# A four-deep ring of decays, residual sums in the matrix engine, and a plain fp32 gated layer in a Mamba block

## The reference, cut to what matters

```python
# x: (8, 512, 128) float32; D_INNER = 256, D_STATE = 16, DT_RANK = 64, HIDDEN = 384
h   = x * rsqrt(mean(x * x) + 1e-5) * norm_w
xs, res = split(h @ in_proj_w.T)
u   = silu(causal_depthwise_conv(xs, taps=4) + conv_b)
delta, Bm, Cm = split(u @ x_proj_w.T, [64, 80])
delta = softplus(delta @ dt_proj_w.T + dt_proj_b)
state[t] = exp(delta * A) * state[t-1] + delta * u * Bm      # 256 x 16 states, over 512 steps
y   = (sum_n state * Cm + u * D) * silu(res)
x1  = layernorm(x + (y @ out_proj_w.T + x))
gate, up = x1 @ w_gate.T, x1 @ w_up.T                         # int weights, scaled by 1/127
out = layernorm(x1 + (silu(gate) * up) @ w_down.T)
```

## Time and profile before

| what | us |
|---|---|
| median of three runs (609.94 to 611.24) | 610.42 |
| the profiled execution's own time | 610.23 |
| its span in the trace | 608.5 |
| DVE busy | 534.5 (88% of the span) |
| PE busy | 425.8 (70%) |
| POOL busy | 398.3 (65%) |
| ACT busy | 355.9 (58%) |
| mean granted TensorE clock | 0.838 of full |

### The profile page before, as it was taken

How to read it: one execution, slowest core, us unless ns; L and a number is a source line. 1 busy time by engine, 2 the same in 40 slices (tenths; PEclk the granted TensorE clock), 3 DMA queues, 4 the chain that set the end, 5 groups by cost and what they waited for, 6 DMA issues and landing times.

```text
span 608.5 us, 5732 instructions
## 1 busy us (share of the span) xinstructions
PE 425.8 (70%) x1477; PEld 172.9 (28%) x1477; DVE 534.5 (88%) x582; ACT 355.9 (58%) x594; POOL 398.3 (65%) x176
## 2 busy tenths in 40 slices
PE   4898586786598595887598695887597694467353
PEld 3332121322232241323232241322242241113142
DVE  4779997989998998989998999989998999999822
ACT  2675874496547675496547775497537774443221
POOL 5588597567776777576776688566776688575000
PEclk9988886997988987987988787987988787777756
DMA  8084044300660044400560043400660044400000
GB/s 213 2 180 98 0 89 95 93 1 1 137 152 5 1 99 80 114 0 0 138 151 4 0 97 93 103 0 0 138 155 0 0 99 92 103 1 0 17 1 18
DMA packets 27360, 39.11 MB, mean 64 GB/s; under 512 B 3816, under 2 KB 10056, under 8 KB 27344
## 3 DMA queue, kind: packets, MB, share of 16 engines
q1 hardware_dynamic: 25424, 38.51, 28.0%
q10 hardware_dynamic: 1920, 0.42, 0.4%
HBM read 3.27 MB, written 2.10 MB: 9 GB/s over the span
## 4 chain that ended last, share of the span: by engine, by line
DVE 37%; issue 22%; POOL 16%; PE 10%; ACT 7%; SPq 4%; DMA 3%; DVEq 1%; POOLq 0%; ACTq 0%
DVE state L904 19%; POOL prod L742 11%; DVE weighted L913 9%; SPq L326 4%; DMA du_rep<-z_wm 2%; PE dense_ps L449 2%; DVE g L920 1%; POOL rs L762 1%; ACT decay_ps L554 1%; DVE g_act L955 1%; PE dense_ps L447 1%; PE y_ps L427 1%; ACT L578 1%; ACT x L565 1%; DVE g_act L951 1%
## 5 line engine op out<-in xcount | busy, mean ns | idle before, releaser
L904 DVE TENSOR_TENSOR_SCAN state<-decay_ps,prod 128x512 f32<-128x512 f32 x256 | 299.2, 1208 | 32.1 <-ACT decay_ps L554 16.7
L742 POOL TENSOR_TENSOR prod<-du_rep,b_rep 128x2048 f32<-128x2048 f32 x63 | 284.8, 4530 | 41.5 <-DVE state L904 35.7
L554 ACT ACTIVATE decay_ps<-delta_rep,a_neg 128x512 f32<-128x512 f32 x252 | 169.8, 687 | 74.6 <-DVE state L904 74.2
L913 DVE TENSOR_TENSOR weighted<-state,c_ps 128x2048 f32<-128x2048 f32 x64 | 146.4, 2287 | 2.7 <-DVE state L904 0.6
L416 PE MATMUL c_ps<-xd,pick 96*128 96x512 f32 x128 | 84.4, 747 | 86.3 <-DVE weighted L913 86.3
L427 PE MATMUL y_ps<-weighted,gather 128*32 128x512 f32 x512 | 87.2, 760 | 6.4 <-DVE weighted L913 6.4
L762 POOL TENSOR_TENSOR rs<-ve,powm 128x4 f32<-128x4 f32 x16 | 16.2, 1012 | 104.5 <-ACT nm L560 104.5
L447 PE MATMUL dense_ps<-h_t,tap_t 128*128 128x512 f32 x128 | 58.9, 604 | 6.5 <-ACT h_t L599 6.5
L416 PEld LDWEIGHTS c_ps<-xd,pick 96*128 96x128 f32 x128 | 25.0, 222 | 120.0 <-DVE weighted L913 111.9
L559 ACT ACTIVATE ve<-mv 128x4 f32<-128x4 f32 x16 | 3.3, 206 | 71.4 <-DVE mv L939 44.1
L746 POOL TENSOR_TENSOR z_wm<-z_e,z_wm 128x512 f32<-128x512 f32 x15 | 18.7, 1269 | 30.3 <-ACT z_wm L622 25.3
(11 more groups left out here) (125 smaller groups left out, 550.0 us busy)
## 6 DMA issues: line engine op xcount, KB each, us to landing
du_rep<-z_wm SPq DMA_DIRECT2D x64, 256.0 KB, 5.0
delta_rep<-z_ln SPq DMA_DIRECT2D x64, 256.0 KB, 4.8
out_dram<-y_out SPq DMA_DIRECT2D x8, 256.0 KB, 4.6
state<-L_attn_in_proj_w_in ACTq DMA_DIRECT2D x1, 256.0 KB, 4.1
x_all<-L_attn_x_in SPq DMA_DIRECT2D x1, 256.0 KB, 4.5
weighted<-L_ffn_w_gate_in SPq DMA_DIRECT2D x1, 192.0 KB, 10.7
weighted<-L_ffn_w_up_in SPq DMA_DIRECT2D x1, 192.0 KB, 4.3
weighted<-L_ffn_w_down_in SPq DMA_DIRECT2D x1, 192.0 KB, 5.1
```

The source lines that it names most:

```text
L554: A(decay_ps[n % DECAYS][:, :], decay_ps[n % DECAYS][:, :] if spread_first else delta_rep[:, h, c, :], ACT.Exp, scale=a_neg[:, col:col + 1 ...
L742: TT(prod[quad % 2][:, :, :], du_rep[:, h, :, :], b, ALU.mult).then_inc(prod_ready, 1)
L904: dve.tensor_tensor_scan(state[:, n % BLOCKS, :], decay_ps[n % DECAYS][:, :], prod[n // BLOCKS % 2][:, n % BLOCKS, :], 0.0, ALU.mult, ALU. ...
L913: TT(weighted[quad % 2][:, :, :], state[:, :, :], c_ps[:, :].unsqueeze(1).broadcast_to([P, BLOCKS, T]), ALU.mult).then_inc(weighted_ready, 1)
```

## The change

Seven edits. (1) The ring has four places; the fourth, for groups with n % 4 = 3 (the last of each quad, since 32 is a multiple of 4), is `decay_sb` in SBUF. (2) 2x is added by PE, a matmul of a matrix `twice` (2 on the diagonal) with x into the projection's bank; ACT copies the sum to `r1` at step 6, DVE takes statistics at step 7 (after group 7) and aggregates at 8, ACT's `shift_scale` is at step 9. (3) `down` is one job in one bank with x1 added by a matmul with the identity, and `down_t` is scaled when it is made; statistics and the last normalisation read PSUM, and r2 is gone. (4) Gate and up take x1 whole in fp32, so `x1_hi`, `x1_lo` and L943 are gone. (5) In the first pass POOL does `soften` and `scale_u` of half 1 of sample 0 after the multiply of quad 2 and not before the first products. (6) ACT's `late_copies` follow group 1 and not 0, and decay 3 is spread into the first bank ahead of C. (7) POOL's `scale_shift` of the first norm comes after multiply 3 and not 2. The state buffer stays single.

```diff
 EPS = 1e-5
-DECAYS = 3
+DECAYS = 4
...
     out_t = sb("out_t", [P, HALVES, M])
-    gate_t = sb("gate_t", [M, HID, P], f32r)
-    up_t = sb("up_t", [M, HID, P], f32r)
+    gate_t = sb("gate_t", [M, HID, P])
+    up_t = sb("up_t", [M, HID, P])
...
-    decay_ps = [pb(f"decay_ps{i}") for i in range(DECAYS)]
+    decay_ps = [pb(f"decay_ps{i}") for i in range(DECAYS - 1)]
+    decay = decay_ps + [sb("decay_sb", [P, T])]
...
             ["C", "S", "up2", "b0", "b1"],
-            ["C", "S", "down0", "down1", "b2", "b3"],
+            ["C", "S", "down", "b2", "b3"],
...
-            "down0": 0, "down1": 1, "b2": 2, "b3": 0}
+            "down": 0, "b2": 1, "b3": 2}
     ALL_JOBS = [name for quad in PLAN for name in quad if name in BANK]
-    OUT_JOBS = [n for n in ALL_JOBS if n in ("proj", "x1") or n[:-1] in ("gate", "up", "down")]
+    OUT_JOBS = [n for n in ALL_JOBS if n in ("proj", "x1", "down") or n[:-1] in ("gate", "up")]
...
                 pe.wait_ge(wt_taken, 4 + n)
-            if n >= DECAYS:
-                pe.wait_ge(scanned, n - DECAYS + 1)
-            mm(decay_ps[n % DECAYS][:, :], spread[:, n, :], delta[:, 0, :], start=True, stop=True
+            if n == 3:
+                pe.wait_ge(scanned, 1)
+            mm(decay_ps[n % 3][:, :], spread[:, n, :], delta[:, 0, :], start=True, stop=True
...
                     for h in range(HALVES):
-                        last = mm(ps[:, i * P:(i + 1) * P], g[:, h, i * P:(i + 1) * P],
-                                  out_t[:, h, :], start=(h == 0), stop=(h == HALVES - 1))
+                        mm(ps[:, i * P:(i + 1) * P], g[:, h, i * P:(i + 1) * P], out_t[:, h, :],
+                           start=(h == 0), stop=False)
+                    at = (it.k0 - 1 + it.ahead) * TILES + i
+                    xk = x_all[:, at, :] if isinstance(at, int) else x_all[:, bass.ds(at, 1), :]
+                    last = mm(ps[:, i * P:(i + 1) * P], twice[:, :], xk, start=False, stop=True)
...
-                    it.wait(pe, x1_hi_ready, 1, -1, 1)
                     it.wait_taken(pe, "x1")
-                w = (gate_t if kind == "gate" else up_t)[:, n, :]
-                mm(ps[:, :], w, x1_hi[:, :], start=True, stop=False)
-                last = mm(ps[:, :], w, x1_lo[:, :], start=False, stop=True)
+                last = mm(ps[:, :], (gate_t if kind == "gate" else up_t)[:, n, :], x1_t[:, :], start=True, stop=True)
             elif kind == "down":
                 it.wait_taken(pe, f"up{HID - 1}")
-                for i in range(2):
+                for i in range(TILES):
                     for b in range(HID):
-                        last = mm(ps[:, i * P:(i + 1) * P], g_act[:, b, (2 * n + i) * P:(2 * n + i + 1) * P],
-                                  down_t[:, b, :], start=(b == 0), stop=(b == HID - 1))
+                        mm(ps[:, i * P:(i + 1) * P], g_act[:, b, i * P:(i + 1) * P], down_t[:, b, :],
+                           start=(b == 0), stop=False)
+                    last = mm(ps[:, i * P:(i + 1) * P], ident[:, :], x1[:, i, :], start=False, stop=True)
...
             if it.k0 == 0:
+                spread_delta(3)
...
                 act.wait_ge(delta_spread, n + 1)
+            if it.k0 == 0 and n == BLOCKS:
+                act.wait_ge(decay_ready, BLOCKS)
...
-            A(decay_ps[n % DECAYS][:, :], decay_ps[n % DECAYS][:, :] if spread_first else delta_rep[:, h, c, :],
+            A(decay[n % DECAYS][:, :], decay_ps[n % 3][:, :] if spread_first else delta_rep[:, h, c, :],
...
             if it.outs:
-                if step == 8:
+                if step == 6:
+                    it.wait_full(act, "proj")
+                    it.take(A(r1[:, :, :], it.ps("proj")[:, :].rearrange("p (i m) -> p i m", m=M), ACT.Copy), "proj")
+                if step == 9:
                     shift_scale(it, mv1, mv1_ready, ve1, nm1, ve1_ready)
                 if step == 12:
-                    normalise(it, x1, r1, rs1, nmr1, shift1_ready, x1_ready)
+                    normalise(it, x1, lambda i: r1[:, i, :], rs1, nmr1, shift1_ready).then_inc(x1_ready, 1)
                 if step == 16:
                     it.wait_full(act, "x1")
-                    A(x1_hi[:, :], it.ps("x1")[:, :], ACT.Copy).then_inc(x1_hi_ready, 1)
+                    it.take(A(x1_t[:, :], it.ps("x1")[:, :], ACT.Copy), "x1")
...
                     act.wait_ge(y_free[it.next], 16 + 16 * ((it.k0 - 1) // 2) + 8 * it.ahead)
-                    normalise(it, y_out[it.next], r2, rs2, nmr2, shift2_ready, y_ready)
+                    ps = it.ps("down")
+                    it.take(normalise(it, y_out[it.next], lambda i: ps[:, i * P:(i + 1) * P], rs2, nmr2,
+                                      shift2_ready), "down")
...
                     exp_decay(it, n + 1)
-                if it.k0 == 0 and n == 0:
+                if it.k0 == 0 and n == 1:
...
                 error(it, 1)
-                soften(it, 1)
-                scale_u(it, 1)
...
                     multiply(it, quad)
-                if it.outs and quad == 2:
+                    if it.k0 == 0 and quad == 2:
+                        soften(Iteration(-1), 1)
+                        scale_u(Iteration(-1), 1)
+                if it.outs and quad == 3:
...
                 it.wait(dve, prod_ready, QUADS, 0, n // BLOCKS + 1)
-            dve.tensor_tensor_scan(state[:, n % BLOCKS, :], decay_ps[n % DECAYS][:, :],
+            dve.tensor_tensor_scan(state[:, n % BLOCKS, :], decay[n % DECAYS][:, :],
...
                     combine(it, 1, -1)
-                if step == 6:
-                    it.wait_full(dve, "proj")
-                    lo = (it.k0 - 1 + it.ahead) * TILES
-                    xk = x_all[:, lo:lo + TILES, :] if isinstance(lo, int) else x_all[:, bass.ds(lo, TILES), :]
-                    it.take(STT(out=r1[:, :, :], in0=xk, scalar=2.0,
-                                in1=it.ps("proj")[:, :].rearrange("p (i m) -> p i m", m=M),
-                                op0=ALU.mult, op1=ALU.add), "proj")
+                if step == 7:
...
-                if step == 7:
+                if step == 8:
...
-                if step == 16:
-                    it.wait(dve, x1_hi_ready, 1, -1, 1)
-                    it.take(TT(x1_lo[:, :], it.ps("x1")[:, :], x1_hi[:, :].bitcast(f32), ALU.subtract), "x1")
...
                                     in1=it.ps(f"gate{b}")[:, :], op0=ALU.add, op1=ALU.mult), f"gate{b}")
-                if step in (26, 27):
-                    n = step - 26
-                    it.wait_full(dve, f"down{n}")
-                    it.take(STT(out=r2[:, 2 * n:2 * n + 2, :],
-                                in0=it.ps(f"down{n}")[:, 0:2 * M].rearrange("p (i m) -> p i m", m=M),
-                                scalar=SILU2, in1=x1[:, 2 * n:2 * n + 2, :],
-                                op0=ALU.mult, op1=ALU.add), f"down{n}")
                 if step == 27:
-                    for n in range(2):
-                        it.wait_taken(dve, f"down{n}")
+                    it.wait_full(dve, "down")
                     for i in range(TILES):
-                        last = dve.bn_stats(st2[:, i, :], r2[:, i, :])
+                        last = dve.bn_stats(st2[:, i, :], it.ps("down")[:, i * P:(i + 1) * P])
```

More of the change, by code:

```diff
@@ L81, in mamba_swiglu_postln @@
         ident = sb("ident", [P, P])
+        twice = sb("twice", [P, P])
         pick = sb("pick", [XC, 2 * CHUNKS, P])
@@ L335, in iteration @@
                 if it.outs:
-                    done, row = value(it.count(1, -1, 1)), value((it.k0 - 1 + it.ahead) * T)
+                    done, row = value(it.job_count("down")[1]), value((it.k0 - 1 + it.ahead) * T)
                 if it.ins:
@@ L357, in iteration @@
                     rows = y_rows[row:row + T, :] if isinstance(row, int) else y_rows[bass.ds(row, T), :]
-                    sp.wait_ge(y_ready, done)
+                    sp.wait_ge(taken[BANK["down"]], done)
                     sp.dma_start(rows.rearrange("(i t) m -> t i m", t=P), y_out[it.next][:, :, :]
@@ L516, in iteration @@
                                 spread_c(it, quad)
-                            if it.k0 == 0 and quad == 0:
-                                spread_delta(DECAYS)
                         elif name == "S":
@@ L560, in shift_scale, with normalise @@
                 A(nm[:, :], mv[:, :, 0], ACT.Copy, scale=-1.0).then_inc(ve_ready, 1)
[L562 removed]
+            def normalise(it, dst, r, rs, nmr, shift_ready):
                 it.wait(act, shift_ready, 1, -1, 1)
                 for i in range(TILES):
[L565 to L566 removed]
+                    last = A(dst[:, i, :], r(i), ACT.Identity, scale=rs[:, i:i + 1], bias=nmr[:, i:i + 1])
+                return last
             def scale_x(it):
@@ L844, in late_setup @@
                     last = TS(skip_t[:, h, :], ident[:, :], dsk[:, h:h + 1], None, ALU.mult)
-                last.then_inc(skip_ready, 1)
```

(5 more changed lines are left out.)

21 lines of the change are left out of this document (8 added, 13 removed).

## The result

| kernel | median, us | range, runs | ratio to before, 95% interval |
|---|---|---|---|
| before | 610.18 | 609.9 to 611.24, 4 | |
| changed | 647.09 | 646.19 to 649.52, 4 | 1.0608 (1.0576 to 1.0639) |

The change costs 37 us, 6%. I had forecast 636 with a range of 606 to 645: the direction and the mechanism came, the size was 11 us short, 2 us above the range.

A forecast was written before the change was run, and what follows sets the result against it. DVE was taken to set the pace, with two chains ending at groups 12 and 0. To 610.2, first pass +7, six passes +18, pass 7 -1.6 and tail +3 gave 636.6, taken as 636; range 606 to 645.

The forecast's parts named there:

- Without contention: Whole kernel if SBUF scans and POOL don't hold each other up: 604.3 us; as rival (DVE not held up), chance 0.18.
- I take 0.54: Each pass, at group 12: moving r1 from DVE to PE keeps 0.54 us of the 0.67 saved.
- 0.58 ... - 0.15: Each pass: dropping x1_lo from DVE gains 0.58 us; PE's third gate in plain fp32 loses 0.15.
- I take the upper end, by the third case: decay_sb scans beside POOL multiplies wait for all that is left, as one DVE L826 waited 0.35 us for POOL's memset.
- Wait 1.7, 2.0, 4.3: Waits in us of the last scans meeting POOL's multiplies in a loop pass: groups 3, 27 and 31 respectively.
- the first of my two cases: At group 31, quad 0's multiply goes first: group 3 is then clear of quad 1's multiply, and the pass takes 71.9 us.
- +3.3 the one way, +3.0 the other: +18 for six passes: Loop: port waits add 3.3 us a pass with the multiply first at group 31, 3.0 with the scan first; +18 altogether.
- the case that never came: At group 31, the scan goes before quad 0's multiply: group 3 of the next pass waits 1.7; the pass takes 71.2 us.
- First pass "+7": First pass: group 3 falls into the early multiply, delaying softening, transfers and quad 4: +4.6 us at group 16, +7 at its end.
- the early gain is gone at group 16: First pass: later softening starts the first products 3.8 us earlier, lost by group 16; some 0.5 us stays.
- Tail "+3": Tail: more projection and fp32 matmuls, less what L943 and r2 give back, make it 3 us longer (2 to 4).
- the likeliest case: The port costs as worked out at groups 27 and 31 and in the first pass: 636 us, 624 to 646, chance 0.68.

The follow-up runs named there:

- the ring of three: The changed kernel with three decays, all in PSUM, and all other edits kept, so no scan reads two SBUF operands; 604.91 us, ratio 0.9918.
- pieces: The changed kernel with POOL's multiply of a quad as four instructions of 128 x 512, not one of 128 x 2048; 621.92 us, ratio 1.0183.
- the first place: The changed kernel with the SBUF decay at the first group of each quad, not the last; 690.37 us, ratio 1.1306.
- the changed order at group 31: The changed kernel, with POOL's multiply of the next sample's quad 0 waiting until all 32 groups are scanned, not 28; 637.88 us, ratio 1.0439.
- Moving `proj`: The changed kernel with PE doing the proj job behind the C matmuls of quad 1, not ahead of them; 642.85 us, ratio 1.0524.

## Why the prediction was wrong in size

**Without contention: right.** "610.2 - 0.5 - 6 - 2.4 + 3 = 604.3"; the ring of three took 604.91. That it came within 0.6 is in part luck, since errors in the terms cancel. By its trace, the head, the first and the six passes together gained 7.1 us (last `weighted` of pass 6 at 500.09, before 507.23), where I had 6.5; pass 7 gained 1.6, not 2.4; the tail lost 1.9, not 3. In the steps, "I take 0.54" for r1 was half its size (1.1 a pass), and the wait before group 12, at the end of the chain through ACT, is shorter with it (1.2 for 1.8). "0.58 ... - 0.15" for x1_lo and the third gate was right (0.42, from one trace of each). The ring itself I had at nothing in the loop: the wait before group 12 is 1.23 with four buffers and 1.19 with three, but a gain hidden in the 42 us wasn't measured apart.

**"I take the upper end, by the third case": right.** The scan waits for all that is left of the multiply, and ends 1.08 or 1.09 behind its end in the rows shown. Three PSUM buffers, pieces, the first place and the changed order at group 31 each moved the time as that says. The Trainium skill, SBUF — State Buffer, section Who interferes with whom, has this rule: of a DVE instruction with two SBUF inputs and a POOL instruction that reads SBUF, the one that issues second is blocked until the first is through. By it the other sum of the prediction, without contention, falls away for this kernel; every run here that keeps `decay_sb` agrees, with an excess from 17 us (pieces) to 93 (first place).

**"Wait 1.7, 2.0, 4.3": right in two.** Group 27 waited 2.0 (3.19 and 3.13 against 1.2) and group 31 4.2. The multiply was always first, so group 3 was free, as in the first of my two cases. I gave 71.9 us for that pass; four of the six took 71.8 to 72.3.

**"+3.3 the one way, +3.0 the other: +18 for six passes": this step failed.** Two things are wrong in it.
- 71.9 less 68.25 is 3.65, not 3.3, and the sum took the 3.0 of the case that never came. With 3.65 it is +22, of the +27.2 measured.
- In two of six passes DVE waited 2.1 us for the C of quad 1, group 23, which I had "just done", waited 0.7, and the pass took 74.7: +5.4 for both. The taps took 5.79 us there and not 3.67: the granted clock was 0.50 over their first 4.2 us, and 1.00 over the taps from 186.69. `proj`, longer by the matmuls with `twice`, stood between them and C. I had looked at PE's clock at the third gate alone. Moving `proj` removes these passes, and so does a shorter wait at group 31. That a long wait of DVE leaves PE idle just before, 10.3 us here, does not decide by itself: before 186.69 it idled as long and ran at full clock, and in the ring of three the taps took 5.80 us in one pass behind only 6.0 us of idling. Why two passes of six stays open.

With the 3.65 the prediction's sum is 640.5, inside its range. The two long passes (+5.4), the head and first pass (2.2 more than forecast), pass 7 (0.6 more) and the tail (1.6 less) bring it to the 647.1 measured. Without the long passes it would have stayed in the range (641.7 by this reckoning; 642.85 was measured with `proj` moved).

**First pass "+7": close.** Head and first pass came to +9.2. Group 16 started at 73.00, forecast "about 73", but behind it groups 19, 23 and 27 took 1.48, 2.13 and 3.60 (the prediction's list, made from a pass of the loop, has 19 and 23 as free). In the trace with the ring of three this pass also shows that "the early gain is gone at group 16" was optimistic: the late softening loses 2.6 us there.

**Tail "+3": too much.** It was +1.4. Pass 7 gained 1.0, forecast 1.6.

The range ended at 645 since the likeliest case ended at 646. Its upper part held only the waits' own bounds, and no second-order effect of them on PE.

## What to carry to other kernels

An operand's memory is a property of the order as well: before a buffer moves from PSUM to SBUF, list for each instruction that reads it what POOL runs at that moment, for every pair of places, back-to-back ones too, and price each with what is left of POOL's instruction. If such an instruction got long with no idle time before it, compare the end of the longest ones with the ends on the other engine. Where the two can't be kept apart, shorter instructions on the other engine bound the wait: four pieces in place of one took two thirds of the excess away. POOL's multiplies got 48 us longer in all by it (333.0 for 285.2, waits for scans included) and its busy time rose by 34 us, which it had to spare.
